# Relation sums of a graph kernel: twelve chunks gathered in twelve partial heights by GpSimd, the rest row by row by SyncE

## What is computed

```python
msg = h[edge_src] * edge_norm[:, None]
agg = jax.ops.segment_sum(msg, edge_rel * N + edge_dst, num_segments=R * N)
out = jnp.einsum('rnbi,rbio->nbo', agg.reshape(R, N, 8, 32), W)
```

## Time and profile before

| | us |
|---|---|
| three runs | 3316.3, 3314.28, 3305.43 |
| median | 3314.28 |
| span of the profiled execution | 3318.0 |

### The profile page before, as it was taken

The page is one execution under the profiler, slowest core; times in us unless marked ns, Lnnn a source line. Parts: engine busy times, 40 slices in busy tenths (PEclk is TensorE's granted clock), DMA queues, the critical chain, the costliest instruction groups (busy, mean ns, idle before and its releaser), DMA issues. The chain is left out here.

```text
span 3318.0 us, 73877 instructions
## 1 busy us (share of the span) xinstructions
PE 2189.3 (66%) x11487; PEld 1592.8 (48%) x11488; DVE 2090.3 (63%) x5467; ACT 1413.4 (43%) x4736; POOL 2386.1 (72%) x2419
## 2 busy tenths in 40 slices
PE   6566377776656367766696666676666677666667
PEld 2455255555455355555443444454444456444446
DVE  8899867766489967776694444464444454444446
ACT  2666399998566479988581000031000014000004
POOL 7877777777777767777655777775777773777773
PEclk9799699998889789999797778687777798777788
DMA  5488734443688745443694333443333332333332
GB/s 165 132 228 226 215 111 141 140 127 105 174 227 227 214 118 163 142 130 104 161 283 159 109 109 109 125 125 108 109 109 109 108 104 78 110 109 110 109 107 79
DMA packets 346744, 466.05 MB, mean 140 GB/s; under 512 B 111879, under 2 KB 262248, under 8 KB 343184
## 3 DMA queue, kind: packets, MB, share of 16 engines
q0 software_dynamic: 111952, 284.59, 29.8%
q1 hardware_dynamic: 161584, 111.23, 11.5%
q10 hardware_dynamic: 72852, 67.08, 7.5%
HBM read 385.50 MB, written 76.97 MB: 139 GB/s over the span
## 5 line engine op out<-in xcount | busy, mean ns | idle before, releaser
L400 PE MATMUL t_ps<-t_ring,shared 128*128 x2640 | 900.5, 494 | 499.2 <-ACTq L237 418.3
L400 PEld LDWEIGHTS t_ps<-t_ring,shared 128*128 128x128 f32 x2640 | 601.8, 244 | 787.5 <-issue 697.4
L186 POOL DMA_INDIRECT ring<-feat_d,srcC x784 | 772.3, 985 | 264.8 <-issue 215.2
L186 POOL DMA_INDIRECT t_ring<-feat_d,srcC x758 | 719.7, 950 | 289.3 <-issue 215.5
L265 ACT ACTIVATE ring<-ring,exC 128x64 f32<-128x64 f32 x3136 | 788.0, 335 | 0.2
L400 PE MATMUL bank<-ring,arena 128*128 x1408 | 426.9, 428 | 166.7 <-ACT ring L265 117.8
L318 DVE TENSOR_TENSOR acc<-acc,t_ps 128x256 f32 x440 | 185.3, 421 | 504.3 <-PE t_ps L400 502.9
L608 POOL DMA_INDIRECT attr_d<-abuf,attr_pos x392 | 401.9, 1025 | 117.7 <-issue 117.7
L186 POOL DMA_INDIRECT t_ring<-rel_d,relC x379 | 360.0, 950 | 160.6 <-issue 107.4
L302 DVE TENSOR_SCALAR shared<-lane,dlocT,weightT 128x128 f32<-128x128 f32 x1320 | 406.4, 360 | 50.9 <-issue 31.9
L1828 ACT COPY t_ring<-t_pt 128x512 f32<-128x512 f32 (+1 forms) x14 | 7.8, 554 | 883.3 <-PE t_pt L1795 883.3
(11 more groups left out here) (297 smaller groups left out, 2715.3 us busy)
## 6 DMA issues: line engine op xcount, KB each, us to landing
arena<-lo_d ACTq DMA_DIRECT2D x392, 128.0 KB
rel_d<-mid_stage SPq DMA_DIRECT2D x25, 1024.0 KB, 4.7
arena<-attr_d SPq DMA_DIRECT2D x98, 260.0 KB, 2.9
abuf<-in_attr SPq DMA_DIRECT2D x56, 448.0 KB
t_ring<-feat_d SPq DMA_DIRECT2D x1536, 1.0 KB
t_ring<-feat_d ACTq DMA_DIRECT2D x1536, 1.0 KB
ring<-feat_d,srcC POOLq DMA_INDIRECT x784
t_ring<-rel_d SPq DMA_DIRECT2D x768, 1.0 KB
```

The lines of the kernel that those rows point to most:

```text
L186: pool.indirect_dma_start(out=ring[:, u % RING, j, 0:D], out_offset=None, in_=table, in_offset=bass.IndirectOffsetOnAxis(ap=index[:, u, j: ...
L400: last = pe.matmul(ps[k % len(ps)][:, 0:g.width], hot[:, k % NHOT, j, :], ring[:, slot, j, 0:g.width], start=(j == 0), stop=(j == 1))
```

## The change

In the relation stage alone GpSimd again issues the second chunk of the twelve pairs, though not in full: the first 127 rows of the first of them, 126 of the second, then 125, 124, 122, 120, 112, 96, 64, 113, 48 and 32 (`PART_ROWS`, 1209 rows in all). SyncE fetches the rows left over, 1, 2, 3, 4, 6, 8, 16, 32, 64, 15, 80 and 96 (327 in all), as single rows. ScalarE fetches none there. The two convolutions' stages keep the old way.

```diff
+PART_ROWS = (127, 126, 125, 124, 122, 120, 112, 96, 64, 113, 48, 32)
...
-def pool_chunks(u, gat, by_row):
+def pool_chunks(u, gat, by_row, partly):
 
-    return 1 if u in by_row or (u == PAIRS - 1 and not gat) else 2
+    return 1 if (u in by_row and not partly) or (u == PAIRS - 1 and not gat) else 2
...
-            for j in range(pool_chunks(u, g.gat, g.by_row)):
+            for j in range(pool_chunks(u, g.gat, g.by_row, g.partly)):
+                h = g.partly[g.by_row.index(u)] if j and g.partly and u in g.by_row else P
                 pool.indirect_dma_start(
-                    out=ring[:, u % RING, j, 0:D], out_offset=None, in_=table,
-                    in_offset=bass.IndirectOffsetOnAxis(ap=index[:, u, j:j + 1], axis=0),
+                    out=ring[0:h, u % RING, j, 0:D], out_offset=None, in_=table,
+                    in_offset=bass.IndirectOffsetOnAxis(ap=index[0:h, u, j:j + 1], axis=0),
                 ).then_inc(pair_landed[u % RING].sem, 16)
...
+    def rows_in(g, n):
+
+        return 16 * sum(P - g.partly[m] if g.partly else P for m in range(n % 2, n + 1, 2))
+
     def sp_gather_rows(sp, tag, g, table, index, ring):
 
         for n, u in enumerate(g.by_row):
+            first, end = (g.partly[n], P) if g.partly else (0, SP_ROWS)
             if u >= RING:
                 sp.wait_ge(g.slot_free, u - RING + 1 + RELEASE)
             if n >= 2:
-                sp.wait_ge(g.rows_landed[n % 2], 16 * P * (n // 2))
-            for q in range(0, SP_ROWS, ROW_REGS):
-                w = min(ROW_REGS, SP_ROWS - q)
+                sp.wait_ge(g.rows_landed[n % 2], rows_in(g, n - 2))
+            for q in range(first, end, ROW_REGS):
+                w = min(ROW_REGS, end - q)
...
             if u in g.by_row:
                 n = g.by_row.index(u)
-                act.wait_ge(g.rows_landed[n % 2], 16 * P * (n // 2 + 1))
+                act.wait_ge(g.rows_landed[n % 2], rows_in(g, n))
             act.sem_inc(g.pair_ready, 1)
             n, share = u // ROW_STEP, u % ROW_STEP
-            if n < len(g.by_row):
+            if n < len(g.by_row) and not g.partly:
...
-        g_rel = Steps("agr", life, False, by_row=BY_ROW)
+        g_rel = Steps("agr", life, False, by_row=BY_ROW, partly=PART_ROWS)
```

More of the change, by code:

```diff
@@ L156, in gnn_program, with __init__ @@
     class Steps:
-        def __init__(self, tag, scope, gat, attr=None, signals=sem, by_row=()):
+        def __init__(self, tag, scope, gat, attr=None, signals=sem, by_row=(), partly=()):
+            self.partly = partly
             self.gat, self.attr, self.width = gat, attr, W_GAT if gat else D
@@ L177, in __init__ @@
                 at = pair_landed[u % RING]
-                at.at += 16 * pool_chunks(u, gat, by_row)
+                at.at += 16 * pool_chunks(u, gat, by_row, partly)
                 self.landed.append(at.at)
```

## The result

The changed kernel takes 3332.26 us (median of 4 runs, 3329.18 to 3333.82) against 3311.03 us before: ratio 1.0066 [1.0051, 1.008], 21.2 us. The forecast was 3328 us in a range of 3319 to 3353, slower.

A forecast was written before the change was run, and what follows sets the result against it. GpSimd's gathers were taken to bound the relation stage; twelve partial ones add 14 us, single rows off ScalarE and SyncE's chunks 0, so 3314.3 + 14 = 3328 us (+0.42%), range 3319 to 3353.

The forecast's parts named there:

- over 1.3 us: Sign that the forecast is wrong: a partial gather on GpSimd in the relation stage taking over 1.3 us.
- GpSimd sets the pace of the stage: Relation stage: GpSimd's gathers, 1.255 us from one to the next, set the pace; TensorE follows.
- twelve more gathers go straight to the end: Relation stage: 379 gathers become 391; the whole shift, taken as +14 us, passes to TensorE's last step.
- Single rows off ScalarE: Relation stage: ScalarE no longer issues 768 single rows; not on the path, worth 0.
- SyncE's uneven chunks: Relation stage: SyncE's 768 rows become 327, largest chunks 80 and 96 rows; hidden, 0.
- the 2179 forecast: SyncE's weight loads, behind its single rows, would end at about 2179 us, before their first user at 2206.64.
- The cost of a partial gather: GpSimd, relation stage: twelve partial gathers add +12.5 (by rows), +13.4 (part fixed) or +15.1 us (flat); taken as +14.
- the adding gather: Gather that adds to its target, 1541 ns against 947; read as 4.6 ns a row and 353 ns fixed.
- Rival A: GpSimd's gathers of heights not splitting by sixteen use fewer engines, 74 ns a turn: 3351 us; chance 24%.
- Rival B: 127 rows on one engine land in 7.1 us; if GpSimd waits for draining, 3335 to 3370 us; chance 6%.
- Rivals C and D: Relation stage: C (6%), TensorE's late steps set end, 3312 to 3317 us; D (2%), SyncE's rows late, 3330 to 3340.
- the forecast's own list: Three values for the twelve partial gathers on GpSimd: +12.5, +13.4 and +15.1 us.

The follow-up runs named there:

- e1: Kernel before, with the twelve relation-stage chunks gathered whole (128 rows) by GpSimd and no single rows there: 3323.45 us, ratio 1.004.
- e2: Changed kernel with its seven awkward heights replaced by 112 rows, SyncE fetching the rest: 3326.58 us, ratio 1.005 to the kernel before.
- e4: Changed kernel with heights 119, 17, 102, 34, 117, 8, 85, 51, 100, 68, 88, 72: 3326.02 us, one run.
- e3: Changed kernel with all twelve heights 127, SyncE fetching one row each: 3345.12 us, ratio 1.0105 to the kernel before.

## Why the prediction was right, point by point

It was right in the direction, in the path by which GpSimd's time reaches the end, and in the range. Its forecast of how long a partial gather takes was not: "over 1.3 us" was its own sign of being wrong, and the gathers of 127, 113 and 122 rows took 2.56, 2.36 and 1.68 us.

- *GpSimd sets the pace of the stage, and twelve more gathers go straight to the end*: right. 12 gathers more, and the time of e1 (12 x 1.255 = 15.1 worked out, 15.4 measured in the stage, 13.8 between the medians).
- *Single rows off ScalarE, worth 0; SyncE's uneven chunks, hidden*: right. SyncE's last row came at 2164.4 and its weight loads ended at 2172.7, 6 us before the 2179 forecast. e1 and e2 show that it doesn't matter who fetches.
- *The cost of a partial gather*: this is the term that was mis-sized, +13.4 to +15.1 us, taken as 14, where the twelve gathers measure 15.8 us busy and 3.6 us of gaps, 19.4, and the stage 20.4 (the other 379 gathers took 361.0 us instead of 360.0). It failed twice. The fixed part was taken as 353 ns from the adding gather, and is about 845 ns, so the five heights that divide by 16 saved 0.2 us in all; 32 rows took 0.87 us and not 0.50. And seven heights don't divide by 16: these cost 4.7 us more than seven full ones, 127 and 113 rows 3.0 of that. The part of the sum that grows came out near by luck: 1209 rows at 4.64 ns are 5.6 us, 396 turns at 13.3 ns 5.3.
- *Rival A, awkward heights dear*: its mechanism is what happened, with a turn priced between five and six times too high, and the fixed part too low. The turns counted (127, 9, 25, 31, 61, 8, 7, 6, 4, 113, 3, 2) give the durations to within 0.11 us, but a turn costs 13.3 ns ((2.56 - 0.947)/(127 - 8) = 13.6, and 0.077/6 = 12.8 from 128 to 32 rows) and not 74. The adding gather was no measure of a turn; what its 594 ns more are spent on stays open. In the Trainium skill, "DMA: Bandwidth & Descriptors" (Why a DMA increments its semaphore by 16 and not by 1) the number of engines is the largest divisor of the slowest dimension up to 16. The seven heights of e4, with seven different divisors and one duration, are what that rule gives for GpSimd's gathers. The trace agrees also by the late updates of the semaphore, k of sixteen (one for 127 rows, five for 125, seven for 119). No run here shows the exception.
- *Rival B*: its delay of 7 us at TensorE came, 5.5 us of it in the landing, free as it was said to be while GpSimd sets the pace; its clogging of GpSimd didn't (e3).
- *Rivals C and D*: no. TensorE waits inside its late steps, the last time at 2243.85, and SyncE's last row was out 22 us before GpSimd's gather of the same pair (2186.23).

Without A the forecast's own list ended at +15.1 us, which the stage's 20.4 lies beyond. The range held because A, kept as a rival at 24%, set its upper end. With the right fixed part and the right price of a turn the sum would have been 12 x 0.845 + 396 x 0.0133 + 3.6 = 19.0 us instead of 14, against 19.4 measured.

## What to carry to other kernels

An indirect gather on GpSimd costs by the call, not by the row: 0.95 us for 128 rows, 0.87 for 32, and 2.56 for 127. Give it a height that is a multiple of 16, or pad it, and save calls rather than rows. Before moving more work to a queue that only issues, add up what its issues and register loads take: the busy share doesn't show it. ScalarE, with 9% of its time left here, had no room for 17% more rows, and what it lacked added up over all fourteen chunks of a stage.

## What the runs showed of the hardware that was not expected

- GpSimd's time for a gather of h rows of 1 KB is 0.845 us + 13.3 ns x h/k, k the largest divisor of h up to 16, within 0.04 us for 22 of the 25 heights run (8 to 128 rows; 127 by the median of its thirteen) and 0.12 us for 126, 125 and 120.
- A load of 32 registers from SBUF takes 2.0 to 2.2 us on ScalarE's queue when it begins on a multiple of 16 bytes (bytes 256, 288 and 304 of the index row) and 6.8 to 7.1 us when it begins at byte 280 or 292. SyncE's loads in the changed kernel part in the same way. The Trainium skill, "Runtime: NRT & Kernel Launch" (Instruction fetch mechanics), has about 200 ns a register even in bulk, and the page speaks of loads from HBM; 6.8 to 7.1 us over 32 are 213 to 222 ns, near that figure, and 2.05 us are a third of it.
- ScalarE starts a single-row DMA every 0.318 us at best, and about every 0.39 us with the loads of row addresses, where the profile lists the issue alone with 0.228 us.
